# Merging the spilled key and query rows into two tensors, with one load each, and halving the weight-conversion pieces

## Reference

```python
h_in = layer_norm(x)
q, k, v = split(h_in @ in_w.T)                 # 16 heads of 64
k = (1 - s) * k + s * k_prev                   # s = sigmoid(smear) per head
logits = q @ k.T * 64 ** -0.5 + slopes * position + causal
o = softmax(logits) @ v
x = layernorm(x + layer_norm(o @ out_w.T))
x = layernorm(x + (silu(x @ wg.T) * (x @ wu.T)) @ wd.T)   # int32 weights / 127
```

## Time and profile before

| | us |
|---|---|
| median of 2 runs | 9059.09 |
| lowest and highest | 9001.47, 9116.72 |
| the profiled execution's own time | 9001.47 |
| its span on the slowest core (core 3) | 8999.9 |
| spans of the eight cores | 8948.4 to 8999.9 |
| TensorE matmul busy | 5442.7 (60%) |

### The profile page before, as it was taken

How to read it: one execution, slowest core, us unless ns; L and a number is a source line. 1 busy time by engine, 2 the same in 40 slices (tenths; PEclk the granted TensorE clock), 3 DMA queues, 4 the chain that set the end, 5 groups by cost and what they waited for, 6 DMA issues and landing times.

```text
span 8999.9 us, 57410 instructions; the slowest of 8 cores (8948.4 to 8999.9 us)
## 1 busy us (share of the span) xinstructions
PE 5442.7 (60%) x13984; PEld 1945.7 (22%) x13984; DVE 1810.6 (20%) x3430; ACT 1119.4 (12%) x1652; POOL 391.2 (4%) x572
## 2 busy tenths in 40 slices
PE   4767463745465456445554556687676676676675
PEld 2323121212122112111111111222222222222221
DVE  3233131313121122111111111111301311311301
ACT  0000000000000110112222222232000000000000
POOL 0000101010000000000000000000000000000000
PEclk7888676877677777677777777888776776776876
DMA  2222212221212112111111121222111111111110
GB/s 61 73 66 66 65 43 62 60 68 40 64 49 71 51 32 72 51 51 42 42 51 47 47 49 36 51 55 57 32 44 53 33 44 55 31 44 54 33 44 27
DMA packets 556190, 453.61 MB, mean 50 GB/s; under 512 B 225492, under 2 KB 487380, under 8 KB 552664
## 3 DMA queue, kind: packets, MB, share of 16 engines
q1 hardware_dynamic: 487712, 316.96, 12.9%
q0 software_dynamic: 31104, 90.48, 3.9%
q10 hardware_dynamic: 37064, 42.50, 1.6%
HBM read 371.69 MB, written 78.14 MB: 50 GB/s over the span
## 4 chain that ended last, share of the span: by engine, by line
PE 50%; DMA 20%; DVE 16%; issue 8%; ACT 4%; DVEq 1%; ACTq 0%; POOLq 0%; SPq 0%; POOL 0%
PE pb L623 12%; PE pb L347 9%; PE pb L872 7%; DMA vbuf<-vspill 6%; DMA wdb_s<-wdb 4%; PE pb L822 4%; PE pb L833 4%; PE pb L590 3%; PE pb L593 3%; DVE rs_s L636 2%; PE pb L746 2%; ACT pbuf L615 2%; PE pb L686 2%; DMA kspl<-ksml 2%; DMA qbufA<-qsph 1%
## 5 line engine op out<-in xcount | busy, mean ns | idle before, releaser
L347 PE MATMUL pb<-xt,wi_s 128*128 128x512 f32 (+1 forms) x2688 | 1334.8, 660 | 338.1 <-DVE xt L329 231.8
L623 PE MATMUL pb<-pbuf,vbuf 128*65 128x512 f32 x2560 | 1410.4, 634 | 200.9 <-ACT pbuf L615 193.0
L590 PE MATMUL pb<-qbufA,kbufA 128*128 128x512 bf16 x1280 | 531.5, 415 | 1441.6 <-DMA qbufB<-qaux 1441.6
L615 ACT ACTIVATE pbuf<-pb,consts 128x512 f32<-128x512 f32 x1280 | 879.4, 687 | 2841.4 <-PE pb L593 1895.9
L347 PEld LDWEIGHTS pb<-xt,wi_s 128*128 128x128 f32 x2688 | 565.3, 218 | 1071.0 <-issue 1067.0
L872 PE MATMUL pb<-hh_s,wdb_s 128*128 128x512 bf16 x768 | 435.5, 567 | 479.4 <-DMA wdb_s<-wdb 432.7
L590 PEld LDWEIGHTS pb<-qbufA,kbufA 128*128 128x128 bf16 x1280 | 132.2, 103 | 1925.8 <-issue 1925.8
L593 PE MATMUL pb<-qbufB,kbufB 68*128 68x512 bf16 x1280 | 534.9, 418 | 0.0
L610 DVE TENSOR_TENSOR pb<-pb,maskA 128x128 f32<-128x128 f32 x256 | 76.8, 300 | 1994.9 <-PE pb L593 1946.8
L623 PEld LDWEIGHTS pb<-pbuf,vbuf 128*65 128x65 f32 x2560 | 327.3, 145 | 663.9 <-issue 526.6
L872 PE MATMUL pb<-hl_s,wdb_s 128*128 128x512 bf16 x768 | 443.3, 577 | 0.0
(11 more groups left out here) (109 smaller groups left out, 3442.0 us busy)
## 6 DMA issues: line engine op xcount, KB each, us to landing
wi_s<-winT SPq DMA_DIRECT2D x168, 512.0 KB, 4.2
wgb_s<-wgb SPq DMA_DIRECT2D x96, 256.0 KB, 3.1
wub_s<-wub SPq DMA_DIRECT2D x96, 256.0 KB, 3.0
wdb_s<-wdb SPq DMA_DIRECT2D x192, 128.0 KB, 2.1
xt<-xT SPq DMA_DIRECT2D x8, 2048.0 KB, 11.3
vspill<-vtstage POOLq DMA_DIRECT2D x128, 128.0 KB, 2.4
kbufA<-ksph SPq DMA_DIRECT2D x32, 512.0 KB
vbuf<-vspill POOLq DMA_DIRECT2D x32, 512.0 KB, 6.5
```

What stands on the lines that cost most here:

```text
L347: e.matmul(pb[bank][:, 0:nw], wi_s[wsl][:, kc * 128:(kc + 1) * 128], buf[:, kc * nw:(kc + 1) * nw], start=(kc == 0), stop=(kc == 7))
L590: e.matmul(pb[sbk][:, :], kbufA[bi][:, j * 128:(j + 1) * 128], qbufA[bi][:, :], start=True, stop=False)
L615: P.step("scalar", (lambda e, sbk=sbk: e.activation(pbuf[sbk][:], pb[sbk][:], AF.Exp, bias=consts[:, 1:2])), waits=[("pe", pe_s), ("dv", d ...
L623: P.step("tensor", (lambda e, j=j, sbk=sbk, bi=bi, njt=njt: e.matmul(pb[2][0:65, :], vbuf[bi][:, j * 65:j * 65 + 65], pbuf[sbk][:], start= ...
```

## The change

The four spilled key and query tensors and the two row tables become four tensors laid out as the attention step wants them: `kspA` has per head 128 rows (the high part twice), `kspB` per head 68 rows (4 table rows, then the low part), `qspA` per head 128 rows (high, low), `qspB` per head 68 rows (4 table rows, then the high part). So the producer stores three pieces per chunk and the consumer loads two. The scratch rows of the start get a place of their own and are made in two halves. The conversion pieces are half as wide, and there are two of them per attention step.

```diff
-    ksph = nc.dram_tensor("ksph", [H * 64, L], BF16_, kind=spk).ap()
-    kspl = nc.dram_tensor("kspl", [H * 64, L], BF16_, kind=spk).ap()
-    kaux = nc.dram_tensor("kaux", [H * 4, L], BF16_, kind=spk).ap()
+    kspA = nc.dram_tensor("kspA", [H * 128, L], BF16_, kind=spk).ap()
+    kspB = nc.dram_tensor("kspB", [H * 68, L], BF16_, kind=spk).ap()
...
+    qspA = nc.dram_tensor("qspA", [H * 128, NQ], BF16_, kind=spk).ap()
+    qspB = nc.dram_tensor("qspB", [H * 68, NQ], BF16_, kind=spk).ap()
...
-    wcv_i = [place(f"wcv_i{i}", [128, FF // 2], I32) for i in range(2)]
+    wcv_i = [place(f"wcv_i{i}", [128, FF // 4], I32) for i in range(2)]
...
+    L2 = L // 2
+    for chh in range(2):
+        cs = slice(chh * L2, (chh + 1) * L2)
+        w0 = [("pre", ld_pre)] if chh == 0 else [("sps", P.c("sps"))]
...
@@ the query stores of a chunk
-                           out=qsph.rearrange("(h r) c -> h r c", r=64)
-                               [2 * oc:2 * oc + 2, :, c0:c0 + nw],
+                           out=qspA.rearrange("(h r) c -> h r c", r=128)
+                               [2 * oc:2 * oc + 2, 0:64, c0:c0 + nw],
                            in_=qsh[:, 0:nw])),
...
+                P.step("scalar", (lambda e, oc=oc, c0=c0, nw=nw:
+                       e.dma_start(
+                           out=qspB.rearrange("(h r) c -> h r c", r=68)
+                               [2 * oc:2 * oc + 2, 4:68, c0:c0 + nw],
+                           in_=qsh[:, 0:nw])),
...
@@ the key stores of a chunk
+                    for dup in range(2):
+                        P.step("scalar", (lambda e, kc_=kc_, c0=c0, nw=nw,
+                                          dup=dup: e.dma_start(
+                               out=kspA.rearrange("(h r) c -> h r c", r=128)
+                                   [2 * kc_:2 * kc_ + 2,
+                                    dup * 64:dup * 64 + 64, c0:c0 + nw],
...
+                               out=kspB.rearrange("(h r) c -> h r c", r=68)
+                                   [2 * kc_:2 * kc_ + 2, 4:68, c0:c0 + nw],
                                in_=ksml[:, 0:nw])),
...
@@ attention step
-        if li < len(conv_tasks):
-            emit_conv(li)
+        for cidx in (2 * li, 2 * li + 1):
+            if cidx < len(conv_tasks):
+                emit_conv(cidx)
...
+            out=kbufA[bi][:, 0:2 * nk].rearrange("p (s c) -> p s c", s=2),
+            in_=kspA[h * 128:h * 128 + 128, :]
...
+            out=kbufB[bi][0:68, 0:2 * nk].rearrange("p (s c) -> p s c", s=2),
+            in_=kspB[h * 68:h * 68 + 68, :]
...
+            out=qbufA[bi][:, :],
+            in_=qspA[h * 128:h * 128 + 128, t * TT:(t + 1) * TT])),
...
+            out=qbufB[bi][0:68, :],
+            in_=qspB[h * 68:h * 68 + 68, t * TT:(t + 1) * TT])),
```

More of the change, by code:

```diff
@@ L163, in build_nc @@
     ostg = place("ostg", [64, TT])
[L164 to L171, removed]
-    wcv_i = [place(f"wcv_i{i}", [128, FF // 2], I32) for i in range(2)]
-    wcv_o = [place(f"wcv_o{i}", [128, FF // 2], BF16) for i in range(2)]
+    ahi16 = place("ahi16", [16, L // 2], BF16)
+    amid16 = place("amid16", [16, L // 2], BF16)
+    alo16 = place("alo16", [16, L // 2], BF16)
+    msl16 = place("msl16", [16, L // 2], BF16)
+    arow = place("arow", [16, L // 2])
+    wcv_i = [place(f"wcv_i{i}", [128, FF // 4], I32) for i in range(2)]
+    wcv_o = [place(f"wcv_o{i}", [128, FF // 4], BF16) for i in range(2)]
     cur[0] = pbase
@@ L225, in build_nc @@
            waits=[("pre", ld_pre)])
-    P.step("vector", lambda e: e.tensor_copy(qposb[:], kpos_s[0:1, 0:NQ]),
+    P.step("vector", lambda e: e.tensor_copy(qposb[:], kpos_s[:, 0:NQ]),
            waits=[("pre", ld_pre)])
     dv_q45 = P.c("dv")
[L229 to L233, removed]
-            waits=[("dv", dv_q45)], dma="sps")
@@ L246, in build_nc @@
[L246 to L254, removed]
+    for rr, tsrc in ((0, qposb), (1, onesb), (2, onesb), (3, onesb)):
+        P.step("scalar", (lambda e, rr=rr, tsrc=tsrc: e.dma_start(
+            out=qspB.rearrange("(h r) c -> h r c", r=68)[:, rr:rr + 1, :],
+            in_=tsrc[:].rearrange("h (r c) -> h r c", r=1))),
+            waits=[("dv", dv_q45)], dma="sps")
@@ new lines, in build_nc @@
+    L2 = L // 2
+    for chh in range(2):
+        cs = slice(chh * L2, (chh + 1) * L2)
+        w0 = [("pre", ld_pre)] if chh == 0 else [("sps", P.c("sps"))]
+        P.step("vector", (lambda e, cs=cs: e.tensor_scalar(
+            arow[:], kpos_s[:, cs], slopes_s[:, 0:1], None, ALU.mult)),
+            waits=w0)
+        P.step("vector", lambda e: e.tensor_copy(ahi16[:], arow[:]))
+        P.step("vector", lambda e: e.tensor_sub(arow[:], arow[:], ahi16[:]))
+        P.step("vector", lambda e: e.tensor_copy(amid16[:], arow[:]))
+        P.step("vector", lambda e: e.tensor_sub(arow[:], arow[:], amid16[:]))
+        P.step("vector", lambda e: e.tensor_copy(alo16[:], arow[:]))
+        P.step("vector", (lambda e, cs=cs: e.tensor_scalar(
+            arow[:], kpos_s[:, cs], 0.0, 1.0, ALU.mult, ALU.add)))
+        P.step("vector", lambda e: e.tensor_scalar(
+            arow[:], arow[:], slopes_s[:, 0:1], -1.0, ALU.mult, ALU.mult))
+        P.step("vector", lambda e: e.tensor_copy(msl16[:], arow[:]))
+        dva = P.c("dv")
+        for rr, tsrc in ((0, msl16), (1, ahi16), (2, amid16), (3, alo16)):
+            P.step("scalar", (lambda e, rr=rr, tsrc=tsrc, cs=cs: e.dma_start(
+                out=kspB.rearrange("(h r) c -> h r c", r=68)[:, rr:rr + 1, cs],
+                in_=tsrc[:].rearrange("h (r c) -> h r c", r=1))),
+                waits=[("dv", dva)], dma="sps")
@@ L486, in build_nc @@
     psS_free = {0: None, 1: None}
[L488 to L490 removed]
+    conv_tasks = ([("g", i, qq) for i in range(8) for qq in range(4)]
+                  + [("u", i, qq) for i in range(8) for qq in range(4)]
+                  + [("d", i, qq) for i in range(24) for qq in range(2)])
     conv_guard = {}
     def emit_conv(idx):
[L494 removed]
+        kind, i, qq = conv_tasks[idx]
         par = idx % 2
```

81 lines of the change are left out of this document (18 added, 63 removed).

## The result

The changed kernel is slower. Over comparable executions of both kernels the ratio of after to before is 1.107, 95% interval 1.098 to 1.117. The profiled execution of after took 9955.38 us, where 9740 was forecast: 954 us more than before's 9001.47, where the forecast said 738.

What follows compares the result with a forecast made beforehand. Stores set the projection's pace, and attention waits on loads queued behind the conversion store, at a fixed price per DMA. 9001.5 + 837 (projection stores) + 8 (start) - 110 (attention) = 9736, rounded to 9740 us; range 9490 to 10080.

Steps and rivals of the forecast that it cites:

- The store's price: Projection, stores of 2 groups of 64 rows: two DMA engines carry each, 4.4 us quiet, 4.9 on average; +837 us together.
- the 0.49 for crowding: Projection key chunks: a store costs 2.39 us on average, 0.49 over the quiet 1.9; added to the broken store's 4.4.
- the rate of `yT`: Projection stores: 23 GB/s per engine, read from the store of yT, so 64 KB on one engine take 2.85 us.
- Other tiles: Key chunks of the four other tiles: period 20.7 us, 604 us in all, so +277.
- Own tiles: Query and key chunks of the four own tiles: query chunk 16.9 us, 280 per tile, 1121 in all, so +560.
- The attention steps: 56 boundaries with conversion: -5.5 for query loads, +3.05 second store, -0.4 cast, +1 order; -1.9 each, -110 us.
- the order on SyncE: Attention boundaries: key loads now stand behind the conversion loads and run beside V; +1 us each, bounds 0 and 5.
- The few tenths for the wider load: Attention, merged query loads: twice the bytes cost a few tenths of a us, taken as within the rounding.
- Start: Tables made in two halves, the second waiting for the first four stores: +8 us, hidden by nothing.
- Even dealing: Rival, projection: stores go over 16 engines whatever the shape, 2.39 us each; 9077 us in all, chance 0.12.
- The slow engine: Rival, projection: stores bound by one engine's slow rate, 7.6 us each; 10450 us in all, chance 0.06.
- Crowded V loads: Rival, attention: key and conversion loads slow both V loads by 2.7 us each; 9967 us in all, chance 0.12.

Runs made afterwards that it cites:

- the crossed runs: The changed kernel with four conversion buffers (9944.6 us), with a semaphore of its own for every second conversion store (9981.8), and with both (four cores 9732 to 9808).
- the fastest version: The kernel before, conversion store moved behind the V and query loads, a semaphore for each of these six loads: ratio to before 0.858, 7730.4 us at best.

## Where the prediction held and where it failed

The direction held, and so did the two mechanisms: two engines carry a broken store, and a second conversion store eats most of what the query loads save. The time was short by 216 us (738 forecast, 954 measured). The step that failed is the price of a broken store, +124 of the miss; the attention steps were forecast too well by 84, start and value chunks by 29, and the last stage came out 20 shorter.

- **The store's price, +124.** The step was "64 KB take 2.85 us and 8 KB took 0.36: 1.9 - 0.36 + 2.85 = 4.4 us quiet, and 4.9 with the 0.49". It measured 4.95 quiet and (22.4 - 6.02)/3 = 5.46 in a key chunk, so the 0.49 for crowding holds (0.51). What doesn't hold is that only the bytes per engine change, and at the rate of `yT`. The packets of a broken store run for 3.40 us, not 2.85, and the first of them starts 0.38 later than that of an even store. I had called the rows of `yT` "of like size", but they are 2 KB, in packets of 2 KB that take 87 ns each, 23 GB/s; the 1 KB packets of the broken store took 56 ns, 18 GB/s, and the 3.40 us come to 19.
- **Where the 124 lie.** Other tiles: 28 key periods of 22.4 for 20.7 are the 49 us missed there. Own tiles, 19 us each: the seven query intervals took 125.3 us where 118.3 was forecast, since the first of them is 20.5 to 21.5 us and the others mostly 17.1 (two stores of the first query chunk at 990 us took 7.1 and 6.6); from the last query copy to the second key copy went 33.6 us for 31.6; and the six key periods after that took 134.0 for 124.2.
- **The attention steps, +84.** The steps were "a store of 256 KB lands in 2.7; I take 2.5 for half, and 0.55 of dispatch: +3.05" and, for the order on SyncE, "I take +1". The second store came 4.27 to 5.64 us after the first, 4.8 in the mean: (4.8 - 3.05) x 56 = 98 us more. The two V loads together were 2.7 us shorter at t = 0 and 0.5 longer at t = 3, -0.7 in the mean instead of +1: 97 us less. These two errors are of one size and cancel, which is luck and has one reason: I had added the order and the store as separate terms, and the crossed runs show that each hides the other. The query loads saved 4.9 to 5.3 us where 5.5 was forecast, and 0.4 to 0.5 came back between the last load and TensorE: 52 us more. The few tenths for the wider load were left out of the sum and belonged in it. The remaining 30 lie in small pieces and outside the boundaries.
- **Start** +11.7 against +8; **value chunks** +25 and **the last stage** -20 against 0. For these no experiment was made; the section on the clock has a row for the value chunks.
- **The rivals.** Even dealing fell (4.95 per store; the run with an even third store shows its price, 179). The slow engine fell (4.95, not 7.6). Crowded V loads gave 9967, which is near what came, but by another road: in after the V loads weren't 2.7 us slower each. Only with the store's wait taken away were the two together 4.8 to 6.2 us slower than before, at t = 2 and 3.

## The clock

Windows (stretch, its length, busy us of PE, PEld, DVE, ACT, POOL with their counts, granted clock, DMA share, GB/s). First before, key chunks of the first of the four other tiles, then the same of after:

```profile
481.90:563.30 81.40, 59.34 (x128) 24.74 (x126) 38.17 (x104) 0.00 (x0) 0.00 (x0) 0.95 0.29 81
```

```profile
664.40:826.60 162.20, 68.36 (x128) 28.27 (x126) 38.20 (x105) 0.00 (x0) 0.00 (x0) 0.73 0.16 46
```

The same 128 matmuls took 59.3 us at a granted 0.95 and 68.4 at 0.73. TensorE was busy for 73% of the stretch before, and 42% after: with more waiting between its bursts the clock granted was lower, not higher. I take it that this cost nothing there, since the stores set the pace. Over the span after has 0.74, before 0.76, and the fastest version 0.80. Whether a wait costs time a second time through the clock no run separates.

The time of the value chunks goes by the clock. One stretch of them in before, then one in after, from the first to the last value copy:

```profile
2742.20:2835.10 92.90, 69.00 (x140) 28.80 (x140) 13.02 (x36) 0.00 (x0) 10.59 (x14) 0.85 0.29 82
```

```profile
4406.00:4509.10 103.10, 79.22 (x140) 32.21 (x140) 13.05 (x36) 0.00 (x0) 10.53 (x14) 0.71 0.22 63
```

Before has a stretch at 0.71, too, of 103.2 us. Over the 64 such stretches of all eight cores the mean is 95.0 us at 0.80 before and 97.7 at 0.78 after, and in either kernel 0.01 of clock goes with some 0.76 us. By that estimate the clock makes about two thirds of the difference; the rest stays open.

## What to carry to other kernels

Before merging or re-laying out a DMA, write down its access list: a store broken into 2 groups of 64 rows cost 4.95 us where one run of 128 rows cost 1.9, and giving each store every second row kept the run whole and won 500 us. If transfers are chained on one semaphore, count them by landing time, and look first at what stands ahead of them in their queue: moving one store behind six loads and giving these their own semaphores was worth 14%, nearly all of it by the store's place, while merging query loads and doubling the conversion stores came to 0.6 us a step. When one cure alone does nothing, cross it with the next one before the cause is dropped.

## What was not expected

- The ACT queue's own instruction is longer for a broken store, 0.50 to 0.61 us against 0.33, its first packet comes 1.16 us after the issue instead of 0.78, and the fixed part of the time grew from 1.54 to 2.1 us.
- A store of half the bytes landed later than the whole one (3.6 against 2.7 us). I take that to be the conversion and key loads that leave SyncE at the same moment; no run shows it.
- Freeing a store of its wait lengthened the second V load by as much as it had won at the boundary shown (6.39 to 12.10 us).
- The granted clock was lower where TensorE was busy for less of the time (0.73 at 42%, 0.95 at 73%).
